# Expert routing in the first mixture of experts: dense products against rows sent to tiles of one expert

## The chip, the cores and the metric

The kernel runs on one core of a Trainium2 chip. The metric is the device time of one execution in microseconds. Half a dozen engines work side by side on one memory (SBUF): TensorE multiplies, VectorE and ScalarE read its results from the banks of PSUM (PB0 to PB7), Pool (GpSimd) helps, and SP issues transfers. They meet by counting semaphores.

## The reference

Four pairs of a convolution-like block and a token block work in turn on x of 8 images, 128 channels and 16x16 positions, that is 2048 tokens of 128 channels. The change is in the first token block, and touches nothing of what is computed. All is fp32.

```python
gate = jax.nn.softmax(xt @ Wg, axis=-1)            # 8 experts
topv, topi = jax.lax.top_k(gate, 2)
topv = topv / (jnp.sum(topv, axis=-1, keepdims=True) + 1e-06)
scores = jnp.zeros((T, E)).at[jnp.arange(T)[:, None], topi].set(topv)
for e in range(E):
    h = jax.nn.gelu(xt @ W1[e] + b1[e], approximate=False)   # 128 -> 512
    ye = h @ W2[e] + b2[e]                                   # 512 -> 128
    out = out + ye * scores[:, e:e + 1]
```

Here xt is the layer-normalised token, and the result is added to the unnormalised one. Two of the eight scores of a token are not zero.

## The kernel before

The tokens stand as 16 tiles of 128 tokens (X: a token on each partition, 128 channels in a row). Four tiles are a slot, and there are four slots. XT holds the normalised tiles, XN the same turned over, channels on the partitions.

First an upsampling and downsampling convolution runs through 28 steps c (TensorE L671 and L681; VectorE L1788, L1797, L1802 on each step). At c = 14, 21 and 28 and at the end VectorE adds a slot's result to X (finish, L1779) and takes its layer-norm statistics (L1688, L1691, L1694); Pool raises them to the power -1/2 (ln_pow, L475), VectorE normalises (L1711), TensorE turns the slot (ln_turn, L630) and ScalarE copies it out (ln_copy, L1352).

Then comes the expert stage. The logits of a token tile are one product with an 8-column matrix (L644). VectorE and ScalarE make scores of them for two slots at a time (router_start, router_act, router_finish: L1725 to L1755, with MAX8 in L1740 and MATCH_REPLACE8 in L1748), which land in comb, a column for each expert. TensorE goes through d = 0 to 31, expert d % 8 on slot d // 8. ffn_up(d) makes four products of 128x128 weights with the slot's 512 columns (L716); ScalarE does the gelu of each (L1402); ffn_down(d) makes, for each of the four token tiles, four 128x128 products (L727). ffn_up(d + 1) stands ahead of ffn_down(d) in the queue. VectorE adds each tile's result times its score to X (L1832), whatever the score is. All the experts' weights lie in SBUF, loaded in one piece at the start (stage1).

In between stand small pieces: the turned scores (comb_turn, L650), the b2 biases as products with them (expert_biases, L738), and the modulation of the next block (L765 to L776, bnrow and bt on ScalarE). After a slot's last expert VectorE takes the statistics for the next block and normalises it; Pool does the power and adds a row to X (shift, L492).

The next block begins with own_heads for three slots (L802, L809), and then takes the projection in which each product reads every sixteenth column of all 2048 tokens (L821). It so needs the last slot to be normalised, turned and copied.

SP issues every load: first (L432), x (L434), later, stage1 and mods (L435 to L437), and then the convolution weights of the later blocks into a ring of four buffers (L445, L447). Pool issues no transfer.

## Time and profile before

| What | us |
|---|---|
| median of 3 runs | 987.94 |
| lowest and highest run | 986.72, 990.4 |
| profiled execution | 988.28 |
| its span in the trace | 986.3 |
| TensorE busy | 842.2 |
| VectorE busy | 572.5 |
| ScalarE busy | 367.1 |
| Pool busy | 197.8 |

The mean granted clock of TensorE is 0.92 of full speed (2.4 GHz); the granted clock of a stretch is a column of the stage table. Busy times are of instructions; issuing a transfer is not in them. The profile names tiles without their numbers, and every tile in the big shared buffer is "arena". An fp32 product is recorded as two instructions. DMA moved 46 MB in 986 us, most of it in the first 40 us and in the two stretches with convolution weights.

### The profile page before, as it was taken

What the parts mean: (1) busy time and instruction counts of PE and PEld (TensorE: products, weight loads), DVE (VectorE), ACT (ScalarE), POOL (GpSimd) and SP (SyncE); (2) the same over time, 40 slices, a digit from 0 to 9 for tenths busy, and PEclk for the clock granted to TensorE, in tenths of its full rate; (3) what the DMA queues carried; (4) which work ended last, traced back from release to release, by engine and by line L of the source; (5) the groups of instructions that cost most, each with busy time, mean ns of one, the idle gap of its engine ahead of it and who ended that gap; (6) DMA issues with size and microseconds to landing.
All of it is one profiled execution on the core that took longest, in us unless ns stands there. A gap on an engine that the chain in (4) does not pass through costs nothing.

```text
span 986.3 us, 13502 instructions
## 1 busy us (share of the span) xinstructions
PE 842.2 (85%) x4689; PEld 636.1 (64%) x4689; DVE 572.5 (58%) x2105; ACT 367.1 (37%) x742; POOL 197.8 (20%) x258
## 2 busy tenths in 40 slices
PE   7999999999999999995866699878877677587868
PEld 5886777777777799985532588645555454363436
DVE  8984222122212345249576403369999989999773
ACT  1005434334333412220100112158868567465321
POOL 4101000010000100002011100235655544443300
PEclk9999999999999999996787799879988879788988
DMA  9600000000000035660000050000000002001020
GB/s 365 263 1 1 1 1 1 1 1 1 1 1 1 0 126 196 243 248 0 1 0 0 1 203 23 1 1 1 1 1 1 1 1 44 0 12 40 17 43 22
DMA packets 6739, 46.00 MB, mean 47 GB/s; under 512 B 632, under 2 KB 1656, under 8 KB 3984
## 3 DMA queue, kind: packets, MB, share of 16 engines
q1 hardware_dynamic: 6672, 45.14, 12.8%
q8 instruction: 38, 0.62, 0.3%
q14 instruction: 29, 0.24, 0.1%
HBM read 44.04 MB, written 1.10 MB: 46 GB/s over the span
## 4 chain that ended last, share of the span: by engine, by line
PE 62%; DVE 22%; issue 7%; POOL 5%; ACT 3%; DMA 0%; DVEq 0%; POOLq 0%; ACTq 0%
PE PB L727 12%; PE PB L716 11%; PE PB L843 5%; PE PB L1029 5%; DVE X L1962 3%; PE PB L681 3%; PE PB L671 3%; POOL arena L622 3%; PE PB L1207 2%; DVE arena L2213 2%; DVE top L2224 2%; PE PB L967 2%; DVE arena L2227 2%; DVE top L2208 2%; PE PB L630 1%
## 5 line engine op out<-in xcount | busy, mean ns | idle before, releaser
L1832 DVE SCALAR_TENSOR_TENSOR X<-PB,comb,X 128x128 f32<-128x128 f32 x128 | 36.0, 344 | 169.9 <-PE PB L727 169.9
L1402 ACT ACTIVATE arena<-PB,arena 128x512 f32<-128x512 f32 x128 | 87.4, 687 | 120.3 <-PE PB L716 120.1
L727 PEld LDWEIGHTS PB<-arena 128*128 128x128 f32 x1024 | 118.5, 192 | 11.0 <-issue 10.4
L727 PE MATMUL PB<-arena 128*128 128x128 f32 x1024 | 119.9, 276 | 0.0
L716 PE MATMUL PB<-XN,arena 128*128 128x512 f32 x256 | 115.6, 594 | 2.2 <-ACT arena L1402 2.2
L622 POOL TENSOR_TENSOR arena<-arena 128x512 f32<-128x512 f32 x64 | 81.3, 1271 | 120.9 <-ACT arena L1656 120.9
L475 POOL TENSOR_TENSOR lnrs<-lnve,mhalf 128x4 f32<-128x4 f32 x20 | 20.4, 1019 | 401.1 <-DVE lnve L1694 401.0
L1116 PE MATMUL PB<-ring 128*128 128x256 f32 x256 | 79.9, 442 | 16.7 <-ACT arena L1648 16.1
L1341 PE MATMUL PB<-w_first,arena 128*128 128x128 f32 x256 | 47.1, 314 | 46.0 <-POOL arena L622 45.6
L1656 ACT ACTIVATE arena<-arena,nmx 128x256 f32<-128x256 f32 x128 | 58.2, 506 | 57.5 <-DVE arena L2227 57.1
L1341 PEld LDWEIGHTS PB<-w_first,arena 128*128 128x128 f32 x256 | 33.2, 159 | 70.7 <-POOL arena L622 64.2
L716 PEld LDWEIGHTS PB<-XN,arena 128*128 128x128 f32 x256 | 46.1, 191 | 49.2 <-issue 44.6
L1116 PEld LDWEIGHTS PB<-ring 128*128 128x128 f32 x256 | 50.6, 219 | 29.8 <-issue 18.9
L1352 ACT ACTIVATE XN<-PB 128x512 f32<-128x512 f32 x20 | 11.9, 595 | 140.4 <-PE PB L630 140.4
L1648 ACT ACTIVATE arena<-PB,nmx 128x256 f32<-128x256 f32 x128 | 53.7, 477 | 5.8 <-DVE nmx L2214 3.8
L843 PE MATMUL PB<-arena,ring 128*128 128x128 f32 x480 | 55.8, 274 | 0.0
L2208 DVE MAX8 top<-PB 128x8 f32<-128x256 f32 x128 | 48.3, 418 | 12.7 <-PE PB L1116 12.6
L843 PEld LDWEIGHTS PB<-arena,ring 128*128 128x128 f32 x480 | 54.7, 190 | 0.0
L2213 DVE MATCH_REPLACE8 arena<-top,PB 128x256 f32<-128x256 f32 x128 | 51.9, 413 | 0.0
L2227 DVE MATCH_REPLACE8 arena<-top,arena 128x256 f32<-128x256 f32 x128 | 51.3, 408 | 0.0
L1029 PEld LDWEIGHTS PB<-arena,ring 128*128 128x128 f32 x392 | 47.5, 200 | 1.5 <-issue 1.5
L1029 PE MATMUL PB<-arena,ring 128*128 128x128 f32 x392 | 48.2, 285 | 0.0
(273 smaller groups left out, 1486.0 us busy)
## 6 DMA issues: line engine op xcount, KB each, us to landing
ring<-in_taps_dram SPq DMA_DIRECT2D x12, 1536.0 KB, 6.9
ring<-in_taps_dram SPq DMA_DIRECT2D x7, 1792.0 KB, 7.3
arena<-in_stage_dram SPq DMA_DIRECT2D x1, 4176.0 KB, 22.7
arena<-comb_rows SPq DMA_DIRECT2D x6, 512.0 KB, 6.2
w_later<-in_later_dram SPq DMA_DIRECT2D x1, 2951.5 KB, 13.3
XN<-in_x_dram SPq DMA_DIRECT2D x4, 256.0 KB, 4.9
out_dram<-XN SPq DMA_DIRECT2D x3, 256.0 KB, 2.2
arena<-in_mods_dram SPq DMA_DIRECT2D x1, 534.0 KB, 23.5
```

What stands on the lines that cost most here:

```text
L622: g.tensor_tensor(PR[c % 2], E1[c % 2], E2[c % 2], ALU.subtract).then_inc(sub_ready, 1)
L716: mm(PB[c % 3][:], W["W1"][:, e, hc * P:hc * P + P], xn(s), start=True, stop=True)\
L727: last = mm(PB[3 + d % 2][:, t * P:t * P + P], H[d % 2][hc][:, t * P:t * P + P], W["W2"][:, d % E, hc, :], start=hc == 0, stop=hc == 3)
L843: last = mm(PB[[3, 6][j % 2]][:, k * P:k * P + P].rearrange("p (b y) -> p b y", b=B), ring[:, j % T_RING, (6 * k + dy) * P:(6 * k + dy) * ...
L1029: last = mm(PB[1 + j % 2][:, k * P:k * P + P].rearrange("p (b y) -> p b y", b=B), ring[:, jj % T_RING, (7 * k + dy) * P:(7 * k + dy) * P + P],
L1116: last = mm(PB[c % 2][:, q * 256:q * 256 + 256], QM[c // 2 % 3][:, o + P * q:o + P * q + P], Kc[:, N * s + HW * j:N * s + HW * j + HW], st ...
L1341: last = tr(PB[3][:, kt * 256 + q * P:kt * 256 + q * P + P], PR[c % 2][:, q * 256 + kt * P:q * 256 + kt * P + P], ident)
L1402: A(H[d % 2][c % 4], PB[c % 3][:], ACT.Gelu, bias=W["b1"][:, c % 32:c % 32 + 1])\
L1656: last = A(E2[c % 2][:, q * 256:q * 256 + 256], REP[c % 2][:, q * 256:q * 256 + 256], ACT.Exp, bias=nmx[c % 4][:, q:q + 1])
L2208: k0 = [mark(v.max(t8[:, q, 0:8], lg[q])) for q in range(2)]
L2213: k.append(mark(v.match_replace(rp[q], t8[:, q, 0:8], lg[q], NEG)))
L2227: last = v.match_replace(rp[q], t8[:, q, 8:16], rp[q], NEG)
```

## The change

Routing is done before the products, and only the chosen experts' products are made. The 16 token tiles are handled as two halves of 8 tiles (two slots each). For each half:

1. pick_experts (VectorE) makes the softmax and finds the best and the second expert of each token as two 0/1 masks, and the two weights. Half 0's stands in the convolution's step c = 27, after logits at c = 20 and 25.
2. ranks (TensorE) counts, by nine products with a triangle of ones and with ones, how many rows before this one chose the same expert. ranks(0) stands after the upsampling steps and ahead of the downsampling left then; ranks(1) ahead of the first tile.
3. place_rows (VectorE, half 0 at c = 28) rounds each expert's count up to full tiles of 128 rows, and gives each of a token's two copies its row number, and each of the ROOM = 23 tiles its expert.
4. scatter (Pool) sends each token tile twice to DRAM, each row to its own row number: 16 indirect transfers for a half. ln_pow(1, 3) stands after the sixth. The DRAM buffers are zeroed by two transfers at the start.
5. SP reads the half's 23 tiles back in one transfer (rows_in), and for every tile reads its expert's number into a register and loads that expert's W1, W2 and b1 (128 x 1028 words) into one of four buffers (expert_weights).
6. For each of the 46 tiles TensorE turns the rows (four tiles or three together), makes four up products and four down products; ScalarE does four gelus of 128 columns. VectorE copies the turned rows and the results, a chunk of four tiles (the sixth of a half has three) at a time, and SP stores each chunk to DRAM.
7. gather (Pool) brings each token tile's two rows back by 16 indirect transfers for a half, and VectorE adds them with their weights (add_rows, 8 operations for a slot). Half 1's stand in two groups of 8, with ln_pow(2, 1) and the shift of slot 0 between, and the shift of slot 1 and the powers and shifts of slots 2 and 3 behind.

The scores in comb, the b2 biases, the modulation and all later stages stay. The loads of stage1 are gone, b2 moved to mods, and mods is loaded before later. Several semaphores of later stages are reused.

The core of the diff, with the repeated renaming left out:

```diff
+HALVES = 2
+HALF = NTOK // HALVES
+HT = HALF // P
+ROOM = 2 * HT + E - 1
+USES = HALVES * ROOM
+CHUNKS = [[list(range(ROOM * h + o, ROOM * h + min(o + 4, ROOM))) for o in range(0, ROOM, 4)] for h in range(HALVES)]
...
-            sp.dma_start(packs["stage1"], a["stage1"]).then_inc(stage1_in, 16)
+            def expert_weights(u):
+                h, i = divmod(u, ROOM)
+                sp.wait_ge(rows_placed, h + 1)
+                if u >= 4:
+                    sp.wait_ge(ffn_down_done, u - 3)
+                e = sp.value_load(tile_expert[0:1, h, i:i + 1], min_val=0, max_val=E - 1)
+                sp.dma_start(WB[u % 4], a["experts"][bass.ds(e, 1)].rearrange("e p w -> (e p) w"))\
+                  .then_inc(weights_in[u % 4], 16)
+
+            def rows_in(h):
+                sp.wait_ge(scattered[h], 2 * HT * 16)
+                sp.dma_start(XG[h], rows_there[h].rearrange("(i p) c -> p i c", p=P)).then_inc(xg_in[h], 16)
...
+            def first_experts():
+                for u in range(4):
+                    expert_weights(u)
+                rows_in(0)
+                for u in range(USES):
+                    if u + 4 < USES:
+                        expert_weights(u + 4)
+                    if u == ROOM - 6:
+                        rows_in(1)
+                    for q in range(len(CHUNKS)):
+                        if u == CHUNKS[q][-1]:
+                            rows_out(q)
...
+            def scatter(t):
+                h = t // HT
+                for k in range(2):
+                    g.indirect_dma_start(rows_there[h], bass.IndirectOffsetOnAxis(ap=row_number[:, h, k, t % HT:t % HT + 1], axis=0),
+                                         XT[:, t, :], None).then_inc(scattered[h], 16)
...
+            pool.wait_ge(zeroed, 16 * HALVES)
+            pool.wait_ge(rows_placed, 1)
+            for t in range(3):
+                scatter(t)
+            ln_pow(1, 3)
+            for t in range(3, HT):
+                scatter(t)
+            pool.wait_ge(rows_placed, 2)
+            for t in range(HT, NT):
+                scatter(t)
...
+            pool.wait_ge(y_stored[1], 16 * PER_HALF)
             pool.wait_ge(setup_act, 3)
+            for t in range(HT, HT + TILES):
+                gather(t)
+            ln_pow(2, 1)
             shift(0, 2, 0, bnrow[:, 1, :])
+            for t in range(HT + TILES, NT):
+                gather(t)
+            shift(0, 2, 1, bnrow[:, 1, :])
+            for s in range(2, SLOTS):
                 ln_pow(2, s)
                 shift(0, 2, s, bnrow[:, 1, :])
...
+            def ranks(h):
+                o = P + 72 * h
+                pe.wait_ge(mods_in, 16)
+                pe.wait_ge(experts_picked, h + 1)
+                m = picked2[:, h]
+                mm(PB[7][:, o:o + 72], W["rows_above"], m, start=True, stop=False)
+                for k in range(1, HT + 1):
+                    last = mm(PB[7][:, o + 8 * k:o + 72], ones[:], m[:, 0:72 - 8 * k], start=False, stop=k == HT)
+                last.then_inc(ranked, 1)
...
+            def ffn_up(u):
+                q = chunk_of(u)
+                i = CHUNKS[q].index(u)
+                pe.wait_ge(xgt_ready, q + 1)
+                pe.wait_ge(weights_in[u % 4], 16 * (u // 4 + 2))
+                if u >= 3:
+                    pe.wait_ge(ffn_gelu_done, u - 2)
                 for hc in range(4):
...
+                    last = mm(PB[u % 3][:, hc * P:hc * P + P], WB[u % 4][:, hc * P:hc * P + P],
+                              XGT[q % 3][:, i * P:i * P + P], start=True, stop=True)
+                last.then_inc(ffn_up_done, 1)
+
+            def ffn_down(u):
+                q = chunk_of(u)
+                i = CHUNKS[q].index(u)
+                pe.wait_ge(ffn_gelu_done, u + 1)
+                if q >= 2:
+                    pe.wait_ge(y_ready, q - 1)
+                for hc in range(4):
+                    last = mm(PB[3 + q % 2][:, i * P:i * P + P], H[u % 3][:, hc * P:hc * P + P],
+                              WB[u % 4][:, HID + hc * P:HID + hc * P + P], start=hc == 0, stop=hc == 3)
                 last.then_inc(ffn_down_done, 1)
```

## Rows read from the trace of the kernel before

**Rows 1.** The page: TensorE busy, with the other engines.

```profile
PE 842.2 (85%) x4689; PEld 636.1 (64%) x4689; DVE 572.5 (58%) x2105; ACT 367.1 (37%) x742; POOL 197.8 (20%) x258
```

**Rows 2.** Chain in order of time: start us, us, what.

```profile
70.25 6.91 PE PB L681 x32
77.60 1.69 PE PB L644 x16
...
150.19 3.57 PE PB L727 x32
153.76 3.44 PE PB L716 x8
...
328.65 10.71 PE PB L821 x32
...
395.32 1.75 PE PB L630 x16
```

**Rows 3.** Stage table: us, busy PE, PEld, DVE, ACT, POOL, clock, DMA share, GB/s.

```profile
78.00:320.00 242.00, 239.82 (x1398) 175.31 (x1398) 58.07 (x260) 99.59 (x148) 10.95 (x20) 1.00 0.00 1
```

**Rows 4.** Groups by form: shapes, count, busy us, mean ns, idle before.

```profile
L1402 ACT ACTIVATE arena<-PB,arena 128x512 f32<-128x512 f32 x128 | 87.4, 687 | 120.3 <-PE PB L716 120.1
...
L1832 DVE SCALAR_TENSOR_TENSOR X<-PB,comb,X 128x128 f32<-128x128 f32 x128 | 36.0, 344 | 169.9 <-PE PB L727 169.9
...
L492 POOL TENSOR_TENSOR X<-X,bnrow 128x128 f32<-128x128 f32 x16 | 6.8, 454 | 36.7 <-ACT bnrow L1393 33.0 <-DVE XT L1711 3.7
...
L1411 ACT ACTIVATE arena<-PB 128x256 f32<-128x256 f32 x8 | 3.1, 383 | 11.1 <-PE PB L802 11.1
```

**Rows 5.** Timeline, VectorE and Pool, 60 to 104 us: start us, us, what.

```profile
75.49 1.11 DVE L1711 TENSOR_SCALAR XT<-X,lnmv,lnrs 128x128 f32<-128x128 f32 x4 [1.12 <-POOL lnrs L475]
...
77.92 0.87 DVE L1688 BATCH_NORM_STATS2 lnst<-X 128x6 f32<-128x128 f32 x4
...
80.40 2.33 DVE L1711 TENSOR_SCALAR XT<-X,lnmv,lnrs 128x128 f32<-128x128 f32 x4 [1.12 <-POOL lnrs L475]
...
86.57 0.65 DVE L1740 MAX8 rt<-rt 128x8 f32<-128x8 f32 x8
...
87.59 0.08 DVE L1748 MATCH_VALUE_LOAD rt<-rt 128x8 f32 x1
...
88.61 0.15 DVE L1748 MATCH_REPLACE8 rt<-rt 128x8 f32<-128x8 f32 x1
...
80.31 1.77 POOL L529 MEMSET arena<- 128x640 f32 x3
```

**Rows 6.** Timeline, SP issuing queue, first 60 us: start us, us, what.

```profile
1.16 1.84 SPq L434 DMA_DIRECT2D XN<-in_x_dram  x4
```

**Rows 7.** DMA issues: count, KB each, median us to landing.

```profile
ring<-in_taps_dram SPq DMA_DIRECT2D x12, 1536.0 KB, 6.9
...
out_dram<-XN SPq DMA_DIRECT2D x3, 256.0 KB, 2.2
arena<-in_mods_dram SPq DMA_DIRECT2D x1, 534.0 KB, 23.5
w_first<-in_first_dram SPq DMA_DIRECT2D x1, 271.0 KB, 2.7
```

**Rows 8.** Groups by form, Pool.

```profile
L622 POOL TENSOR_TENSOR arena<-arena 128x512 f32<-128x512 f32 x64 | 81.3, 1271 | 120.9 <-ACT arena L1656 120.9
...
L475 POOL TENSOR_TENSOR lnrs<-lnve,mhalf 128x4 f32<-128x4 f32 x20 | 20.4, 1019 | 401.1 <-DVE lnve L1694 401.0
```

**Rows 9.** Stage table again, later windows, columns as in rows 3.

```profile
430.00:440.00 10.00, 8.44 (x62) 7.73 (x62) 5.89 (x19) 2.48 (x4) 0.00 (x0) 1.00 0.97 348
...
450.00:452.00 2.00, 0.00 (x0) 0.00 (x0) 2.00 (x1) 0.00 (x0) 0.18 (x1) 0.97 0.00 0
452.00:454.00 2.00, 0.87 (x4) 0.87 (x5) 1.93 (x5) 0.00 (x0) 0.00 (x0) 0.50 0.00 0
...
482.00:484.00 2.00, 1.96 (x7) 0.60 (x5) 1.90 (x18) 0.00 (x0) 0.00 (x0) 0.85 0.00 0
```

More of the change, by code:

```diff
@@ L719, in ffn_down @@
-            def ffn_down(d):
-                pe.wait_ge(ffn_gelu_done, 4 * d + 4)
-                if d < 2:
-                    pe.wait_ge(x_after_conv, 3 + d)
-                else:
-                    pe.wait_ge(ffn_added, d - 1)
-                for t in range(TILES):
-                    for hc in range(4):
-                        last = mm(PB[3 + d % 2][:, t * P:t * P + P], H[d % 2][hc][:, t * P:t * P + P],
-                                  W["W2"][:, d % E, hc, :], start=hc == 0, stop=hc == 3)
+            pe.wait_ge(*at(xn_ready[1], 2))
@@ new lines, in _, with chunk_of, turn_rows @@
+            ln_turn(1, 3, PB[6])
+            logits(0, 1, 2, W["Wg0"], PB[7])
+            logits(0, 1, 3, W["Wg0"], PB[7])
+            pe.wait_ge(x_after_conv, SLOTS)
+            def chunk_of(u):
+                return next(q for q, c in enumerate(CHUNKS) if u in c)
+            def turn_rows(q):
+                h = q // PER_HALF
+                if q == 0:
+                    pe.wait_ge(*at(xn_ready[1], 3))
+                else:
+                    pe.wait_ge(xgt_ready, q)
+                pe.wait_ge(xg_in[h], 16)
+                for i, u in enumerate(CHUNKS[q]):
+                    last = tr(PB[5][:, i * P:i * P + P], XG[h][:, u - ROOM * h, :], ident)
+                last.then_inc(xg_turned, 1)
@@ new lines, in place_rows @@
+            def place_rows(h):
+                o = P + 72 * h
+                tiles, start, end, first = [rank[:, 0, E * i:E * i + E] for i in range(4)]
+                dve.wait_ge(ranked, h + 1)
+                link(v.tensor_scalar(tiles, PB[7][:, o + 64:o + 72], 63.5, 1.0 / P, ALU.add, ALU.mult))
+                link(v.tensor_scalar(tiles, tiles, ROUND, -ROUND, ALU.add, ALU.add))
+                sums = rank[:, 1, 0:E * E].rearrange("p (a b) -> p a b", a=E)
+                link(v.tensor_tensor(sums, W["experts_below"], tiles.unsqueeze(1).to_broadcast([P, E, E]), ALU.mult))
+                link(v.tensor_reduce(start, sums, AX.X, ALU.add))
+                link(v.tensor_scalar(first, start, float(P), None, ALU.mult))
+                link(v.tensor_tensor(rank[:, 2, 0:HT * E].rearrange("p (t e) -> p t e", t=HT),
+                                     PB[7][:, o:o + 64].rearrange("p (t e) -> p t e", t=HT),
+                                     first.unsqueeze(1).to_broadcast([P, HT, E]), ALU.add))
+                link(v.tensor_tensor(rank[:, 3].rearrange("p (k n) -> p k n", k=2), picked[:, h],
+                                     rank[:, 2, 0:HT * E].unsqueeze(1).to_broadcast([P, 2, HT * E]), ALU.mult))
+                link(v.tensor_reduce(rank[:, 4, 0:2 * HT], rank[:, 3].rearrange("p (t e) -> p t e", e=E), AX.X, ALU.add))
+                v.tensor_copy(row_number[:, h].rearrange("p k t -> p (k t)"), rank[:, 4, 0:2 * HT])
+                link(v.tensor_tensor(end, start, tiles, ALU.add))
+                ahead = before.rearrange("p (i e) -> p i e", e=E)
+                link(v.tensor_tensor(ahead, W["tile_number"].unsqueeze(2).to_broadcast([P, ROOM, E]),
+                                     end.unsqueeze(1).to_broadcast([P, ROOM, E]), ALU.is_ge))
+                link(v.tensor_reduce(rank[:, 4, 2 * HT:2 * HT + ROOM], ahead, AX.X, ALU.add))
+                link(v.tensor_scalar(rank[:, 4, 2 * HT:2 * HT + ROOM], rank[:, 4, 2 * HT:2 * HT + ROOM], E - 1.0, None,
+                                     ALU.min))
+                v.tensor_copy(tile_expert[:, h], rank[:, 4, 2 * HT:2 * HT + ROOM]).then_inc(rows_placed, 1)
@@ new lines, in add_rows @@
+            def add_rows(s):
+                dve.wait_ge(gathered[s], 16 * 2 * TILES)
+                done = {}
+                for k in range(2):
+                    for t in range(TILES * s, TILES * s + TILES):
+                        if k:
+                            after(done[t])
+                        done[t] = mark(v.scalar_tensor_tensor(X[:, t, :], G[:, t, k, :],
+                                                              row_weight[:, t // HT, t % HT, k:k + 1], X[:, t, :],
+                                                              ALU.mult, ALU.add))
+                after(done[TILES * s + TILES - 1])
+                ln_stats(2, s)
@@ L1840, in _ @@
+            turned_rows(0)
+            for q in range(len(CHUNKS)):
+                if q + 1 < len(CHUNKS):
+                    turned_rows(q + 1)
+                rows_done(q)
+                if q < SLOTS:
+                    dve.wait_ge(fb_done, q + 1)
+                    k = mark(v.tensor_tensor(xf(q), xf(q), PB[6][:], ALU.add))
                     after(k)
                     v.nop().then_inc(fb_added, 1)
-                if d == 8:
-                    dve.wait_ge(mods_in, 16)
+                if q == 2:
```

466 lines of the change are left out of this document (268 added, 198 removed).

## The prediction

> **What bounds the kernel now.** I read the page first. TensorE is busy for 85% of the span and no other engine for more than 58% [rows 1], but that is a mean over eight stages, so I went to the chain in order of time for the first 460 us [rows 2]. From 70 us to 329 us it is TensorE nearly alone, and from 90 us on it repeats two pieces: 3.57 us of L727 (the down products of one expert on one slot) and 3.44 us of L716 (the up products of the next). There are 32 of each, with small insertions between them, and L821 begins at 328.65 us. The table by stage confirms it: from 78 to 320 us TensorE is busy 239.8 of 242 us at granted clock 1.00 (2.4 GHz), ScalarE 100 us, VectorE 58 us, Pool 11 us, DMA 1 GB/s [rows 3]. So this stage ends when TensorE has done its products, everything else hides in it, and the DMA engines are idle. Of the products three quarters are multiplied by a zero score.
>
> I compare everything at one point, the start of L821, which needs all four slots after the expert stage. It stands at 328.65 us; what follows is not changed but for renamed semaphores, and I cost that at nothing.
>
> **What goes.** 32 pairs, 32 x (3.44 + 3.57) = 224 us of TensorE, and beside them 128 gelus of 512 columns at 0.687 us and 128 VectorE additions of 0.344 us [rows 4]. The last two cost nothing today; TensorE covers them.
>
> **What comes, on TensorE.** A 128x128x128 product in fp32 is two instructions. L727 does 32 instructions in 3.57 us, so a product is 0.223 us. A tile of 128 rows now needs 4 up and 4 down products, 1.79 us, and a transpose, 0.11 us from the 16 of L630 in 1.75 us [rows 2]: 1.9 us. There are 46 tiles (23 in each half, since eight experts can each leave one tile part full), so 87 us instead of 224. The score turns, biases and the modulation products, about 9 us, stay. TensorE alone would need about 97 us.
>
> **What comes around it.** Rows must be sorted before the first tile and fetched back after the last. I follow the path.
>
> (a) *Picking, half 0.* It is put into the convolution's last steps on VectorE, and the rank products stand in TensorE's queue ahead of the last downsampling, so TensorE waits for it. VectorE needs eight MAX8 (0.65), sixteen pairs of value load and MATCH_REPLACE8 (eight of them stand between 87.59 and 88.76 us) [rows 5] and some nine small ops, which I put at 0.2 us each (an estimate from the 0.15 of one MATCH_REPLACE8 on 8 columns): about 5 us to the mask, after its own step at 72 us, so 77 us. The 18 rank instructions cost like the 16 of L644, 0.106 us each [rows 2], 1.9 us, or twice that since the clock will have fallen; done at 80.5. The downsampling of the last slot (6.9 us, L681 [rows 2], longer at the lower clock) then ends near 90 instead of 77 us. That is half 1's trouble and is hidden, for half 0 is not waiting for it. VectorE goes on with statistics (0.87 us [rows 5] and about 0.5 to gather them, 1.4) and fifteen small ops to place the rows, ready at about 85 us.
>
> (b) *Sending half 0.* Sixteen indirect transfers of 128 rows, issued by Pool one after another. The trace has no transfer issued by Pool. Nearest below is what SP's queue takes to issue one, 1.84 / 4 = 0.46 us [rows 6]; above I take the whole 2.2 us from issue to landing of a 256 KB store [rows 7], as if none overlapped. Pool's own instructions give 1.02 us for the power of 4 columns and 1.27 us for a 128x512 tensor op [rows 8]. I take 1.27, because addresses made in software resemble Pool work more than SP's. 16 x 1.27 + 1.0 (a power that stands between) = 21.3, to 106.3 us; landed (2.2) at 108.5.
>
> The Trainium skill, DMA: Bandwidth & Descriptors, Anatomy of one DMA, fits a Pool-issued transfer at 2.0 us and its bytes over 436 GB/s; for 64 KB an estimate of 2.15 us, if none overlapped. By that the sum would be 28 us higher. No run here shows it yet.
>
> (c) *Reading half 0.* SP fetches 23 tiles, 1.5 MB, only after all have landed. The tap loads are of that size, 6.9 us [rows 7]; these come in pieces of 512 bytes, I take 7.5: 116 us. Turn and copy (0.44 + 0.69 + waits): the first up product at 117.7 us.
>
> (d) *Weights.* Each tile has its own expert's 526 KB, loaded into four buffers. Tile u+4's load is issued when tile u's down products are done, so it has the time of four half steps, 4 x 0.893 = 3.6 us, to land. What it takes: a read of the expert's number into an SP register, which nothing here shows (from 0.1 to 2.7 us, the landing of the first pack; I take 1.3, between them), address and issue 0.5, landing 3.5 us (between 2.7 for 271 KB and 6.9 for 1536 KB [rows 7]). That is 5.3 us, late by 1.7, and four tiles share one turn: (5.3 + 3.6 + 0.3) / 4 = 2.3 us a tile. The floor is TensorE's 1.9. 46 x 2.3 = 106 us, at 229 GB/s; a stretch of tap loads ran at 348 GB/s [rows 9], so rate is no limit. ScalarE does four gelus of 128 columns, about 0.27 each from the 0.687 and 0.383 us of 512 and 256 columns [rows 4], 1.1 us a tile, under TensorE's. VectorE only copies, 2 x 0.69 us for four tiles. Half 1's picking, sending and reading lie under half 0's tiles (it has until 158 us and should land near 137). Add 4 us for the parts of the 9 that are not swallowed and 2 for a cold start. The last down product: 229.5 us.
>
> (e) *Fetching back.* Half 0's gathers are hidden. For half 1 the store of the last chunk lands at 233, then Pool issues 8 gathers, a power, four shifts (1.8, L492 [rows 4]), 8 gathers: 16 x 1.27 + 2.8, to 256.1, landed at 258.3. Behind them in Pool's queue stand the powers of slots 2 and 3, for which VectorE and then TensorE wait. VectorE applies slot 2, adds slot 3's rows (8 x 0.33) and its statistics (1.4), Pool's power 1.0, apply 1.1, turn and copy 1.5: L821 begins at about 267.7 us.
>
> (f) *Clock.* TensorE has nothing for some 20 us before its first tile and again at the gathers. In the trace, after a window without work (450 to 452 us), the clock read 0.50 (1.2 GHz) from 452 us, and 0.85 only in the window that begins at 482 us [rows 9]. I add 3 us for the second restart, as if about 6 us of its work ran at 1.2 GHz; by the 30 us of that row it could be 15.
>
> **Sum.** 328.65 - 267.7 = 61, less 3, gives 58 us. The profiled execution took 988.28 us (span 986.3), so 930. The median of the runs, 987.94, is the same within the scatter of 986.72 to 990.4. Thirty-two indirect transfers and forty-six tiles are the multipliers: a microsecond more in each moves the result by 32 or 46. Bounds: 0.46 us a transfer takes 26 off, tiles at 1.95 take 16 off, 888 together; 2.2 us a transfer adds 30, and 960.
>
> **Rivals.**
> *TensorE is the bound* (register read and landing fit into the slack): tiles at 1.95 us, 914; with transfers at 0.8 us, 899. For it: the DMA engines are idle and loads of this size could fly in threes. Chance 15%.
>
> *The weight loads are the bound.* If a load takes as long as a tap load of 1536 KB, because four are in flight beside the scatters, a turn is 6.9 + 1.3 + 3.9 over four, 3.0 us a tile: 34 us more, 964. For it: the stage's mods pack, queued behind others, took 23.5 us to land [rows 7]. Chance 20%. The Trainium skill, DMA: Bandwidth & Descriptors, Rules for kernel authors, speaks against loads this small: it wants 1 MiB and more, since the fixed part of each is paid again. By that rule this rival is the result; no load of this size is in the trace.
>
> *Pool is too slow at addresses, and the kernel ends slower.* Only the two serial trains of 16 decide, and the gain of 58 us is gone at 1.27 + 58 / 32 = 3.1 us a transfer; at 3.5 us the time is 1001. For it: VectorE and Pool disturb each other here, the four normalisations of a slot (L1711) took 2.33 us beside Pool's memsets (from 80.31 us) and 1.11 us otherwise [rows 5], and VectorE is active during both trains. Against: while the tiles run its reads are mostly from PSUM, and the disturbed op only doubled. Chance 6%. The Trainium skill, SBUF — State Buffer, two separate sides, gives such a rule: a Pool-issued transfer of 620 ns took 3100 ns beside a VectorE copy. By that rule this is the result, and the trace agrees in direction.
>
> *The clock falls in the tiles.* If TensorE, busy 1.9 of 2.3 us, is granted 0.50, a tile takes 3.8 us: 69 us more, 999. For it the 30 us at 0.50 above; against, 1.00 with 84% busy from 430 to 440 us [rows 9]. Chance 4%.
>
> **Chances.** Forecast 50%, TensorE-bound 15, weight-bound 20, Pool 6, clock 4, and 5 for mixtures that end near the old time. Half a per cent, 5 us, is about what these measurements can tell. Faster 0.86, same 0.04, slower 0.10. The range 900 to 975 leaves out the cheapest corner and the slower cases.
>
> **What would show it.** Right: the projection that follows (L821 now) starts near 268 us; Pool shows two trains of 16 at about 1.3 us each; the first up product near 118 us; tiles follow every 2.3 us with TensorE waiting for weight DMAs; clock 1.00 inside the tiles. Wrong: the trains at 2 us and more, tiles at 3 us with SP's register read in front, the wait before the last downsampling well above 10 us, or a clock of 0.5 in the tiles.

## The result and the profile after

The changed kernel takes 947.09 us (median of 4 runs, 942.53 to 949.14) beside 987.46 us of the kernel before on the same chip: ratio 0.958, 95% interval 0.954 to 0.962. Forecast were 930 us and a range of 900 to 975. The profiled execution of the changed kernel took 942.53 us, its span is 940.7, and the comparison is made with that one, as the prediction made it with 988.28.

The page of the changed kernel, the row that answers to [rows 1], and the row of the weight loads in its list of DMA issues (count, KB each, median us from issue to landing):

```profile
PE 734.5 (78%) x4227; PEld 578.5 (61%) x4227; DVE 570.7 (61%) x2109; ACT 326.7 (35%) x794; POOL 260.1 (28%) x323
...
arena<-in_experts_dram SPq DMA_DIRECT2D x46, 514.0 KB, 4.5
```

TensorE lost 107.7 us of busy time (842.2 to 734.5) and the kernel 45.8. It is now busy for 78% of the span, not 85.

The lines have moved: the up product L716 is L865, the down product L727 is L876, the transpose of rows is L854, the projection L821 is L958. The chain of waits of the changed kernel in order of time, which answers to [rows 2] (start us, us, what):

```profile
79.35 3.32 PE PB L827 x16
...
87.05 1.25 POOL rows_there L612
88.30 0.30 issue
88.61 0.96 POOL rows_there L612
...
106.12 0.96 POOL rows_there L612
...
107.39 2.23 DMA rows_there<-XT,row_number
...
109.69 8.03 DMA arena<-rows_there
...
117.85 1.10 PE PB L854 x4
...
119.72 3.79 PE PB L865 x16
```

and its end, from the last tile to the projection:

```profile
248.71 2.07 DMA rows_back<-arena
...
272.68 0.94 POOL arena L618
...
273.65 1.68 POOL X L575 x4
275.32 1.02 POOL lnrs L558
...
276.37 1.13 DVE XT L1847 x4
...
286.03 4.24 PE PB L958 x12
```

The chain has fifteen transfers of Pool; the sixteenth is issued at 107.39, and from there the chain goes on with the transfer itself. In place of one even row of products there are now three pieces behind the picking: 33 us of sending and reading (87.05 to 119.72), where TensorE has little to do, 128.4 us of tiles to 248.09, and 37.9 us of fetching back to 286.03. The stage table has one row for the tiles (columns as in [rows 3], where TensorE was busy 239.82 of 242 us at 1.00 and the DMA engines moved 1 GB/s):

```profile
120.00:248.00 128.00, 110.14 (x849) 103.72 (x849) 22.22 (x52) 54.77 (x192) 29.61 (x33) 0.94 0.73 223
```

TensorE is idle for 17.9 of 128 us, its granted clock is 0.94, not 1.00, and the DMA engines, idle before, are busy for 73%. The waits of that stage (engine, line, what it waited for: us in total, times, longest) have no releaser that the profile could name ("issue"); that they are waits for weights is shown by e2_no_loads, below:

```profile
PE PB L865 <- issue: 17.4, 24, 1.9
```

After the projection nothing was changed, and it takes 654.7 us (940.7 - 286.03) in place of 657.65 (986.3 - 328.65).

### The profile page after: what moved, and what is told of

Same layout as the page of the kernel before. It is cut to its first block, busy times and chain, and to the rows that moved or that the text cites. A ratio compares the mean times of both kernels' runs of the same rounds, so it can differ in the third digit from the quotient of the medians.

```text
span 940.7 us, 12950 instructions
## 1 busy us (share of the span) xinstructions
PE 734.5 (78%) x4227; PEld 578.5 (61%) x4227; DVE 570.7 (61%) x2109; ACT 326.7 (35%) x794; POOL 260.1 (28%) x323
## 4 chain that ended last, share of the span: by engine, by line
PE 51%; DVE 30%; issue 7%; POOL 6%; ACT 4%; DMA 2%; DVEq 0%; POOLq 0%; ACTq 0%; SPq 0%
PE PB L980 6%; PE PB L865 6%; PE PB L1166 5%; PE PB L876 5%; DVE arena L2442 3%; DVE X L2191 3%; DVE top L2453 3%; PE PB L786 3%; DVE top L2437 3%; DVE arena L2456 2%; PE PB L796 2%; PE PB L1344 2%; PE PB L1104 2%; POOL arena L618 2%; POOL rows_there L612 2%
## 5 line engine op out<-in xcount | busy, mean ns | idle before, releaser
L1253 PE MATMUL PB<-ring 128*128 128x256 f32 x256 | 76.4, 426 | 17.4 <-ACT arena L1784 16.8
L1534 ACT ACTIVATE arena<-PB,arena 128x128 f32<-128x128 f32 x184 | 52.2, 365 | 73.2 <-PE PB L865 73.2
L865 PE MATMUL PB<-arena 128*128 128x128 f32 x368 | 54.6, 296 | 18.3 <-issue 17.4
L1253 PEld LDWEIGHTS PB<-ring 128*128 128x128 f32 x256 | 48.7, 211 | 29.5 <-issue 18.8
L865 PEld LDWEIGHTS PB<-arena 128*128 128x128 f32 x368 | 48.4, 206 | 23.0 <-issue 19.9
L980 PE MATMUL PB<-arena,ring 128*128 128x128 f32 x480 | 55.7, 274 | 0.0
L980 PEld LDWEIGHTS PB<-arena,ring 128*128 128x128 f32 x480 | 54.7, 190 | 0.0
L745 PE MATMUL PB<-w_first,XT 128*128 128x128 f32 x80 | 18.1, 369 | 45.3 <-DVE XT L1847 44.9
L876 PE MATMUL PB<-arena 128*128 128x128 f32 x368 | 51.7, 286 | 0.3 <-ACT arena L1534 0.3
L618 POOL DMA_INDIRECT arena<-rows_back,row_number x32 | 30.6, 955 | 72.0 <-DMA rows_back<-arena 63.0
L2042 DVE COPY arena<-PB 128x512 f32<-128x512 f32 (+1 forms) x12 | 8.0, 669 | 66.6 <-PE PB L876 66.6
L876 PEld LDWEIGHTS PB<-arena 128*128 128x128 f32 x368 | 47.2, 200 | 1.4 <-ACT arena L1534 0.5
```

Source lines behind the costliest of these rows:

```text
L865: last = mm(PB[u % 3][:, hc * P:hc * P + P], WB[u % 4][:, hc * P:hc * P + P], XGT[q % 3][:, i * P:i * P + P], start=True, stop=True)
L876: last = mm(PB[3 + q % 2][:, i * P:i * P + P], H[u % 3][:, hc * P:hc * P + P], WB[u % 4][:, HID + hc * P:HID + hc * P + P], start=hc == 0, ...
L980: last = mm(PB[[3, 6][j % 2]][:, k * P:k * P + P].rearrange("p (b y) -> p b y", b=B), ring[:, j % T_RING, (6 * k + dy) * P:(6 * k + dy) * ...
L1253: last = mm(PB[c % 2][:, q * 256:q * 256 + 256], QM[c // 2 % 3][:, o + P * q:o + P * q + P], Kc[:, N * s + HW * j:N * s + HW * j + HW], st ...
L1534: last = A(H[u % 3][:, hc * P:hc * P + P], PB[u % 3][:, hc * P:hc * P + P], ACT.Gelu, bias=WB[u % 4][:, 2 * HID + hc:2 * HID + hc + 1])
```

## The experiments

Marks of the profiled executions; "tiles" is from the first up product to the end of the last down product, "tail" from there to the projection, "rest" from there to the end of the span. A ratio is to the kernel before on the same chip.

| kernel | first up | tiles | tail | projection | rest | median us | ratio, 95% interval |
|---|---|---|---|---|---|---|---|
| forecast | 117.7 | 111.8 | 38.2 + 3 | 270.7 | 657.7 | 930 | |
| changed | 119.7 | 128.4 | 37.9 | 286.0 | 654.7 | 947.1 | 0.958 (0.954 to 0.962) |
| e1_again | 119.5 | 128.0 | 37.8 | 285.3 | 663.9 | 945.0 | 0.954 (0.947 to 0.960) |
| e2_no_loads | 119.4 | 101.2 | 37.3 | 257.9 | 659.9 | 918.9 | 0.928 (0.921 to 0.935) |
| e3_six_buffers | 120.2 | 106.1 | 37.9 | 264.1 | 653.6 | 919.7 | 0.932 (0.924 to 0.940) |
| e4_half_trains | 113.1 | 124.7 | 27.5 | 265.3 | 662.4 | 930.3 | 0.940 (0.934 to 0.946) |
| e5_shifts_last | 119.5 | 127.4 | 37.0 | 283.8 | 661.2 | 946.8 | one run |
| e6_kept_busy | 119.8 | 131.5 | 38.3 | 289.6 | 661.4 | 953.0 | one run |
| e7_ranks_late | 119.9 | 128.6 | 38.3 | 286.8 | 662.0 | 950.6 | one run |
| e8_best | 115.0 | 103.1 | 37.0 | 255.1 | 659.3 | 916.3 | 0.928 (0.925 to 0.932) |
| e9_three_buffers | 120.2 | 184.5 | 37.9 | 342.6 | 653.6 | 998.0 | one run |
| e10_best_plain | 115.1 | 104.7 | 37.9 | 257.7 | 650.3 | 916.6 | 0.929 (0.924 to 0.934) |
| e11_best_warm | 117.6 | 107.4 | 37.8 | 262.8 | 660.1 | 923.2 | 0.932 (0.926 to 0.938) |

The stages up to the projection repeat within a microsecond (changed and e1_again, the same code). The rest does not: it runs from 650.3 to 663.9 in kernels that are alike there. So the stages are read at the projection, and the totals are left for what is larger than some 10 us. Where the table says one run, marks and time are of a single execution.

**e1_again.** The changed kernel unchanged.

> The changed kernel once more, to stand beside the next three on one chip. Every theory: 940 to 950 us, first up product near 120 us, last down product near 248 us, 2.8 us a tile.

Measured 945.01 us (940.37 to 951.03), and the marks of the table. The miss against 930 is no accident of one execution.

**e2_no_loads.** Only the first four tiles load weights; the other 42 use what lies in the four buffers, so their products are of the wrong experts. Nothing else is left out; the stores of a half wait for each other.

```diff
                 if u >= 4:
                     sp.wait_ge(ffn_down_done, u - 3)
+                    return
                 e = sp.value_load(tile_expert[0:1, h, i:i + 1], min_val=0, max_val=E - 1)
...
-                pe.wait_ge(weights_in[u % 4], 16 * (u // 4 + 2))
+                pe.wait_ge(weights_in[u % 4], 32)
```

> Only the first four tiles' weights are loaded, every later tile uses those four buffers again; SP keeps its waits. The results are not the reference's. Theory A, the tiles wait for their weights: up products start with no wait, about 2.0 us a tile plus 8 us of other products, some 102 us for the stage instead of 128, total about 920. Theory B, the handshake of TensorE with ScalarE's gelus and VectorE's copies sets the 2.8 us: no change, 942 to 947. Theory C, the clock: with the waits gone the granted clock should be 1.00 from 126 us to the end of the stage.

Measured: tiles in 101.2 us, 27.2 less. The stage table of 100 us of it:

```profile
120.00:220.00 100.00, 99.66 (x845) 97.44 (x844) 22.23 (x52) 54.76 (x192) 28.63 (x33) 0.97 0.21 64
```

TensorE has no gap left, and this is its own price for 46 tiles with all that stands between them: 2.2 us a tile. The 27 us of the changed kernel above it are then 17.9 us of gaps and some 9 us in which TensorE is busy for longer with the same products (110.14 in place of 101). These 9 us have two parts. A clock that is either 1.00 or 0.50 and reads 0.94 on average over 128 us was at half for about 15 us, against 6 us here; the trace puts 13.5 us of the changed kernel's products at half clock and 5.9 us of this one's, which costs some 4 us. And an up group that starts behind a gap stands in the chain with 1.13 us, one that follows without a gap with 0.89. The second can be seen in the changed kernel at 178.26 (its chain), the first in the chain under (d) below:

```profile
178.26 0.89 PE PB L865 x8
```

With 24 gaps that is 24 x 0.24, 6 us. The clock goes with the gaps: 0.97 here, 0.94 in the changed kernel, 0.85 in e9_three_buffers below. Here it is at half only in the first 6 us of the tiles.

**e3_six_buffers.** Two more weight buffers, which take the place of the padded buffers of a later stage (they are cleared behind the last tile, for that). All else is as in the changed kernel.

```diff
-                if u >= 4:
-                    sp.wait_ge(ffn_down_done, u - 3)
+                if u >= 6:
+                    sp.wait_ge(ffn_down_done, u - 5)
...
-                sp.dma_start(WB[u % 4], a["experts"][bass.ds(e, 1)].rearrange("e p w -> (e p) w"))\
+                sp.dma_start(WB[u % 6], a["experts"][bass.ds(e, 1)].rearrange("e p w -> (e p) w"))\
...
```

> Six weight buffers instead of four, in room that is dead while the tiles run; Pool clears the padding buffers after the last tile instead of before the first. Theory A1, the latency of a load with too few in flight: with down(u) behind up(u+1) in the queue, n buffers give (L + 1.8) / (n - 1) a tile; L = 6.1 us gives 2.6 for four and 1.6 for six, so TensorE's 2.0 to 2.1 us sets the pace, stage near 104 us, total about 922. Theory A2, the rate of the DMA engines: a load takes longer in proportion, the tiles stay at 2.6 to 2.8 us, total 940 to 947.

Measured: tiles in 106.1 us, and a median of 919.66 us (916.85 to 928.67). The same loads, of the same bytes, 46 of them, and 22 of the 27 us are back. What remains is in part one wait: the rows of half 1 are asked for at tile 17 and land behind the queued weights. Timeline of TensorE in e3_six_buffers (start us, us, engine, line, operation, tile, the idle time before with what ended it):

```profile
173.20 1.06 PE L868 MATMUL PB<-arena 128*128 128x128 f32 x8
176.89 0.63 PE L857 MATMUL PB<-w_first,arena 128*128 128x128 f32 x4 [2.63 <-DMA arena<-rows_there]
```

**e9_three_buffers.** One buffer fewer, to tell two forms of the cadence apart.

```diff
-                if u >= 4:
-                    sp.wait_ge(ffn_down_done, u - 3)
+                if u >= 3:
+                    sp.wait_ge(ffn_down_done, u - 2)
...
-                sp.dma_start(WB[u % 4], a["experts"][bass.ds(e, 1)].rearrange("e p w -> (e p) w"))\
+                sp.dma_start(WB[u % 3], a["experts"][bass.ds(e, 1)].rearrange("e p w -> (e p) w"))\
...
```

> Three weight buffers in place of four: tile u+3's weights are issued when tile u's down products are done. By the theory (up(u+1) stands in TensorE's queue ahead of down(u), so a buffer's round trip covers n-1 tiles) a tile takes (L + 1.8) / 2; with L, from a buffer free to weights landed, 0.9 + 4.5 = 5.4 to 6.1 us, that is 3.6 to 3.95 us a tile, and the tile stage 166 to 182 us in place of 128; the last down product starts at 285 to 301 us, total 980 to 998. The rival is the prediction's own form, (L + 3.9) / n with n buffers: 3.1 to 3.3 us a tile, stage 143 to 152, last down product at 262 to 271, total 957 to 967. If rate in flight sets L (three loads land faster than four), both lie at their lower ends.

Measured 998.0 us in its one run, above all seven runs of the kernel before beside it (984.4 to 992.7); tiles in 184.5 us, 4.0 us a tile. Its stage table, and its load of the weights in the list of DMA issues:

```profile
120.00:304.00 184.00, 128.19 (x845) 120.24 (x846) 22.33 (x53) 54.76 (x192) 30.01 (x34) 0.85 0.53 158
```

```profile
arena<-in_experts_dram SPq DMA_DIRECT2D x46, 514.0 KB, 3.7
```

The form with n buffers in the denominator allowed 152 us at most and is out. The form with n - 1 came nearer, 2.5 us short at its upper end, but the landing, 3.7 us with fewer loads in flight, was shorter than it assumed: with 3.7 it gives (4.6 + 1.8) / 2 = 3.2 us a tile, the form with n (4.6 + 3.9) / 3 = 2.8. What decides between them is a stretch at full clock. The up groups of TensorE's timeline start at 158.19 and, two tiles later, at 165.22: 7.0 us, of which 0.9 are a turn of rows and one of scores, so 3.1 us a tile. The next two tiles, in part at half clock, take 9.2 us (to 174.44). What the form leaves out is thus the lower clock (in the row above, at 0.85, TensorE's own 101 us became 128), the insertions, and one wait of 6.5 us for a load that was issued beside the read of half 1's rows and took 9.3 us to land.

**e4_half_trains.** Each row is sent to and fetched from its first expert only, 8 transfers in each train in place of 16; its second expert's row is not computed, and the first is added twice. The 46 tiles stay.

```diff
-                for k in range(2):
+                for k in range(1):
                     g.indirect_dma_start(rows_there[h], bass.IndirectOffsetOnAxis(
...
-                for k in range(2):
+                for k in range(1):
                     g.indirect_dma_start(G[:, t, k, :], None, rows_back[h],
...
```

> Only the first of a token's two rows is sent and fetched: 8 indirect transfers in each train instead of 16; VectorE adds the first row twice. The results are not the reference's. Theory: Pool's issue at 1.26 us each is the path, so 8 fewer before the first tile and 8 fewer after the last give 20 us less, about 927, with the first up product near 110 us. Rival: landing and reading back set the path, less than 5 us gained.

Measured: the projection 20.7 us earlier: 10.4 of it in the tail (37.9 to 27.5), 6.6 ahead of the first tile and 3.7 in the tiles, for which no run shows a cause. Behind the tiles the train stands on the path with its full length, as the prediction had it. In front, eight transfers of 1.26 us are 10.1, and the first up product came at 113.1, not near 110. Pool waits 2.21 us for VectorE's variances in the middle of the train, and then something else ends last. TensorE's timeline of e4_half_trains:

```profile
109.27 1.09 PE L854 MATMUL PB<-w_first,arena 128*128 128x128 f32 x4 [0.37 <-DMA arena<-rows_there]
113.13 3.78 PE L865 MATMUL PB<-arena 128*128 128x128 f32 x16 [2.77 <-DVE arena L2034]
```

The rows were turned at 109.27, but VectorE's copy of them (L2034) stands in its queue behind the placing of half 1's rows, which waits for half 1's rank products and ends near 112.5. In the changed kernel that placing is done at 114.8 and the copy starts at 118.97: half 1's picking is hidden there by no more than 4.2 us. By the chain of the changed kernel above, a transfer is 0.96 us of Pool and 0.30 us of issue: 1.26 us, forecast 1.27.

**e5_shifts_last.** Pool's four shifts behind the powers for which VectorE waits.

```diff
             ln_pow(2, 1)
-            shift(0, 2, 0, bnrow[:, 1, :])
             for t in range(HT + TILES, NT):
                 gather(t)
-            shift(0, 2, 1, bnrow[:, 1, :])
-            for s in range(2, SLOTS):
-                ln_pow(2, s)
-                shift(0, 2, s, bnrow[:, 1, :])
+            ln_pow(2, 2)
+            shift(0, 2, 0, bnrow[:, 1, :])
+            ln_pow(2, 3)
+            for s in range(1, SLOTS):
+                shift(0, 2, s, bnrow[:, 1, :])
```

> Pool's four shifts go behind the powers of slots 2 and 3, nothing else is moved. Theory, Pool's queue is the path after the last tile: the second train of eight ends 1.7 us earlier and slot 2's power follows at once, so the projection L958 starts about 3.3 us sooner after the last down product ends than in the changed kernel (there 248.1 to 286.0, 37.9 us; here 34.6). Rival, the arithmetic of VectorE and TensorE is the path there: the distance stays within 0.5 us.

Measured: the tail is 0.9 us shorter. The timelines of e5_shifts_last say where the rest went, Pool first, then VectorE:

```profile
262.27 2.52 POOL L618 DMA_INDIRECT arena<-rows_back,row_number  x1 [0.30 <-issue]
...
272.31 1.04 POOL L558 TENSOR_TENSOR lnrs<-lnve,mhalf 128x4 f32<-128x4 f32 x1
273.34 1.67 POOL L575 TENSOR_TENSOR X<-X,bnrow 128x128 f32<-128x128 f32 x4
```

```profile
261.77 2.18 DVE L2051 SCALAR_TENSOR_TENSOR X<-arena,row_weight,X 128x128 f32<-128x128 f32 x8
...
273.39 2.22 DVE L1847 TENSOR_SCALAR XT<-X,lnmv,lnrs 128x128 f32<-128x128 f32 x4 [8.04 <-POOL lnrs L558]
...
280.23 1.71 DVE L1847 TENSOR_SCALAR XT<-X,lnmv,lnrs 128x128 f32<-128x128 f32 x4 [1.13 <-POOL lnrs L558]
```

The power of slot 2 comes at once behind the last gather (272.31, not behind a shift of 1.68 us), 1.8 us sooner behind the last down product than in the changed kernel, where 3.3 were expected. But then the normalisation L1847 and the shift run side by side, and L1847 takes 2.22 and 1.71 us, where the changed kernel had 1.12 at both places; and one gather took 2.52 us as VectorE's additions began. e10_best_plain, below, is the counterpart.

**e6_kept_busy.** 14 products of constants, never read, ahead of the first turn of rows and ahead of the last slots' turn.

```diff
             ranks(1)
+            for i in range(14):
+                mm(PB[4][:, 0:P], ident, ones[:], start=True, stop=True)
             turn_rows(0)
...
```

> Fourteen idle products (about 6 us at half clock) are put where TensorE waits for the first tile, and fourteen more where it waits for slot 2; their results are not read. Theory, the clock at 1.2 GHz costs time on the path: the first tiles at full clock, 2 to 3 us less before 130 us, and turn, own_heads and the last turn in about 4 us less before the projection. Rival: the clock does not come back in either stretch, and the time stays or grows by up to 1 us.

Measured: no gain, the projection at 289.6 in place of 286.0. The windows of 10 us around the first tile, the changed kernel and then e6_kept_busy:

```profile
110.00:120.00 10.00, 2.57 (x11) 2.10 (x12) 3.74 (x15) 0.00 (x0) 3.83 (x4) 0.50 0.63 170
120.00:130.00 10.00, 10.00 (x69) 9.78 (x70) 0.69 (x1) 5.00 (x17) 7.65 (x8) 0.78 0.37 112
```

```profile
110.00:120.00 10.00, 8.13 (x42) 7.73 (x43) 3.75 (x15) 0.00 (x0) 3.38 (x4) 0.67 0.61 170
120.00:130.00 10.00, 9.96 (x72) 9.51 (x73) 0.69 (x1) 5.00 (x17) 7.55 (x9) 0.84 0.42 131
```

The clock is up from 0.50 to 0.67 and from 0.78 to 0.84, but the first up product came no earlier (119.8) and the tiles were waiting for weights. Of the 3.6 us that the projection came later 3.1 are in the tiles, where the clock reads 0.92 on average against 0.94; with one run it is open whether the idle products did that. The second set did not reach its aim: it ran at 273.98 to 277.27, and TensorE then had nothing for 4.50 us.

**e7_ranks_late.** The rank products of half 0 behind the remaining downsampling, not ahead of it.

```diff
-            ranks(0)
             for s, i in todo:
                 downsample(s, i)
+            ranks(0)
```

> The rank products of half 0 stand behind the rest of the downsampling instead of ahead of it. Theory: the wait of TensorE for the picking (5.6 us before L825) is not on the path, since half 1 has slack, while half 0's placing is: rows placed 1 to 3 us later, and everything to the projection later by as much. Rival, the early ranks cost time because they hold back the last slot: the first tile comes earlier or the stage gets shorter.

Measured: first up product at 119.9, projection at 286.8, in place of 119.7 and 286.0, so neither theory's microseconds: half 0's first scatter begins at 87.20 in place of 87.05. TensorE's 5.64 us of waiting for the picking (row under (a) below) cost nothing, and sparing them gained nothing.

**e8_best.** The six buffers; the rows of half 1 asked for at tile 9; of half 0's rows the first four tiles in a transfer of their own; Pool's order of e5_shifts_last.

```diff
-                    if u == ROOM - 6:
+                    if u == 9:
                         rows_in(1)
...
+                if h == 0:
+                    sp.dma_start(XG[h][:, 0:4, :], rows[:, 0:4, :]).then_inc(x_loaded[2], 16)
+                o = 4 if h == 0 else 0
+                sp.dma_start(XG[h][:, o:, :], rows[:, o:, :]).then_inc(xg_in[h], 16)
```

> Six buffers (e3), half 1 read back at tile 9 instead of 17, half 0's first four tiles read by a transfer of their own, shifts last (e5). Theory: on e3's projection start of 264.2 us, the 10 us gap before half 1 goes, the split read gives 3 to 4 us, the shifts 3 us: about 248 us, total near 905. Rival, the DMA engines are the bound once tiles run at 2 us beside the reads: 255 us or more, total 912 and up.

Measured 916.3 us (913.8 to 920.34), ratio 0.928 (0.925 to 0.932): 30.8 us below the changed kernel's 947.1. The first up product comes 4.7 us earlier, and the wait for half 1's rows is gone. The expected 248 and 905 us were missed by 7 and 11. Against e3_six_buffers the split read and what goes with it gave 5.2 us, the earlier read of half 1 3.0 in the tiles where 10 were put down, and Pool's order 0.9 in place of 3. The numbers are the rival's, 255 and 912 or more, but not its cause: TensorE is idle for 1.8 of the 103 us of tiles, so it is the bound there and not the DMA engines. In front the first tile now waits for what e4_half_trains showed, VectorE's copy behind the placing of half 1's rows. TensorE's timeline of e8_best:

```profile
115.02 3.78 PE L875 MATMUL PB<-arena 128*128 128x128 f32 x16 [2.06 <-DVE arena L2044]
```

That placing ends at 114.4 here. Putting the copy, or the first turn of rows, ahead of half 1's picking was not tried.

**e10_best_plain** and **e11_best_warm.** The first is e8_best with Pool's order of the changed kernel, the second adds both sets of 14 products.

> As e8_best, but with Pool's order behind the tiles as in the changed kernel (each shift where it was). In e5_shifts_last and e8_best one gather took 2.52 us beside VectorE's additions, and the next normalisation 2.2 us beside the shift. If the later shifts give nothing because Pool and VectorE stretch each other, this kernel lies within 2 us of e8_best (914 to 920); the rival is that the new order still gave its 1 to 3 us, so 917 to 923. Last down product near 218 us, projection 37 to 38 us later.

> e10_best_plain with the two sets of 14 idle products on TensorE, ahead of the first turn of rows and behind the last tile's copy (their results are not read). In e6_kept_busy the weight loads set the pace, so a better clock in front had nothing to give; here six buffers leave TensorE as the bound. If the cold start costs here, the first 10 us of tiles go from a granted clock near 0.5 to near 1.0 and 2 to 4 us are gained (912 to 916). The rival: the first tiles still wait for their weights and rows and the second set stands too early in time to help the projection, so no difference within 2 us.

Measured: 916.62 and 923.21 us. Pool's new order gives 0.9 us in the tail (37.0 and 37.9) and nothing that the totals show. Either is the best version found: 31 us below the changed kernel, 71 below the kernel before. e11_best_warm is 6.6 us slower, where 2 to 4 us less or no difference were expected. The idle products cost 2.5 us at the first tile: they ended at 116.4, while in e10_best_plain the rows had landed and were being turned at 112.1. The tiles took 2.7 us more, for which no run shows a cause. TensorE's timeline in e10_best_plain and in e11_best_warm:

```profile
115.08 3.79 PE L875 MATMUL PB<-arena 128*128 128x128 f32 x16 [1.85 <-DVE arena L2044]
```

```profile
111.05 5.33 PE L899 MATMUL PB<-ones,w_first 128*128 128x128 f32 x28
...
117.60 2.05 PE L875 MATMUL PB<-arena 128*128 128x128 f32 x16 [0.78 <-DVE arena L2049]
```

The two first up groups took 2.05 us in place of 3.79, so the cold start costs 1.7 us there, less than the products that end it. With six buffers the DMA engines are busy all the time where weights, stores and Pool's gathers come together, and TensorE even so has no gap; two windows of e10_best_plain:

```profile
190.00:200.00 10.00, 10.00 (x91) 9.91 (x90) 2.02 (x4) 6.16 (x23) 7.56 (x9) 1.00 1.03 377
200.00:210.00 10.00, 10.00 (x91) 10.00 (x91) 1.78 (x3) 5.70 (x20) 1.59 (x2) 1.00 1.00 358
```

Ten loads of weights were issued in these 20 us, 5.3 of the 7.4 MB moved, so about 263 GB/s are weights.

## Why the prediction was right in its sign, and where it was short

Its point, the projection, came at 286.0 and not at 270.7: 15.3 us later; the rest was 3.0 us shorter, which is chance, since that stage runs from 650.3 to 663.9 us; 930 + 15.3 - 3.0 = 942.3, the profiled 942.5. (By the medians the miss is 17 us, within the range given.) Point by point:

*(a) Picking* was forecast with the mask at 77 and the ranks at 80.5 us; L827 ended at 82.67 and the first scatter began at 87.05, forecast 85. The downsampling left then took 8.46 us to 90.97, forecast 90. TensorE's wait was 5.64 us, and e7_ranks_late shows it hidden. That half 1's picking is hidden too holds by 4.2 us alone (e4_half_trains).

```profile
78.68 0.67 PE L825 MATMUL PB<-arena 128*128 128x72 f32 x2 [5.64 <-DVE arena L1923]
82.51 8.46 PE L796 MATMUL PB<-arena 126*128 126x256 f32 x28
```

*(b) Sending* was right: 1.26 us each, the last one issued at 107.39 and landed at 109.6 (forecast 108.5). That it came to the 1.27 of a 128x512 tensor operation is luck in part: the price has two pieces, 0.96 us of Pool, near its small power of 1.02 [rows 8], and 0.30 between two. The Trainium skill, DMA: Bandwidth & Descriptors, Anatomy of one DMA, would have put 28 us on top. Its fixed part is there, since a transfer to DRAM lands 2.23 us after its issue, but the next is issued after 1.26: latency, not occupancy, and e4_half_trains prices a transfer on the path at 10.4 / 8 = 1.3 us.

*(c) Reading half 0* took 8.03 us in place of 7.5, and the first up product came at 119.7 in place of 117.7. e8_best reads what the first four tiles need by itself and starts them 4.7 us earlier.

*(d) Weights* is the step that failed: "(5.3 + 3.6 + 0.3) / 4 = 2.3 us a tile". Measured 128.4 / 46 = 2.79, with insertions; forecast 111.8 / 46 = 2.43 with them. That is 16.6 us. With 2.0 more in front, and 3.3 fewer behind than the 38.2 + 3 put down, it makes the 15.3 at the projection. Of the inputs, the register read was dearer in the forecast (1.3 us) than on the chip (0.27 us and 0.15 us for its two instructions, 0.8 us in all from a down product's end to the issue), and the landing was 4.5 us at the median in place of 3.5 (3.3 at the least, 5.2 in the stretch below, beside the gathers); together they nearly made up for each other at the median, but not beside other traffic. The forecast called a load of this size absent from the trace; the mods pack of 534 KB [rows 7] was one, though queued behind others. What was wrong in kind was the turn. The chain of waits of the changed kernel, with the issues of the queue that reads weights beside it, tells it:

```profile
199.24 0.89 PE PB L876 x8
200.14 0.31 issue
200.45 1.13 PE PB L865 x8
201.58 0.89 PE PB L876 x8
202.47 1.06 issue
203.53 1.13 PE PB L865 x8
204.66 0.44 PE PB L854 x4
205.09 0.89 PE PB L876 x8
205.99 1.03 issue
207.02 1.13 PE PB L865 x8
208.15 0.89 PE PB L876 x8
```

```profile
200.94 0.34 SPq L492 DMA_DIRECT2D arena<-in_experts_dram  x1
```

Call the down product (L876) at 199.24 that of tile v. It ends at 200.13, the load of tile v+4 into its buffer is issued at 200.94, and up(v+4) (L865) starts at 207.02, 6.9 us behind that end (this load took 6.0 us to land). TensorE works in order, and up(u+1) stands ahead of down(u): behind up(v+4) comes down(v+3), which ends at 209.04 and only then frees the next buffer of this turn. From down(v) to down(v+3) are 8.9 us for three tiles, 2.97 each: the round trip, from a buffer free to the products that wait for it (L) and then an up and a down group, is shared by n - 1 tiles, not by n. Here that is (6.9 + 1.13 + 0.89) / 3 = 2.97. With L = 0.8 + 4.5 to 5.2 + 0.1 = 5.4 to 6.1 us it is (5.4 to 6.1 + 1.8) / 3 = 2.4 to 2.6 us without the insertions; the forecast's form gives 2.3 to 2.5 for the same L. With six buffers it is at most 7.9 / 5 = 1.6, below TensorE's 1.9, and the bound goes back to TensorE (e3_six_buffers, e8_best); with three it is 3.2, and e9_three_buffers shows it at full clock.

How the 16.6 us divide can only be estimated from these numbers. The form is worth about 0.1 us a tile with four buffers, 3 to 6 us (with three it is 0.4, which is why e9_three_buffers can tell). The longer round trip of the loads is worth 1 to 9 us. The rest is what the forecast had at nothing: products behind a gap that take 0.24 us longer a group and the part at half clock (9 us of TensorE together, not all of it on the path), and one collision. SP asks for half 1's rows at 172.91, the load issued at 175.49 takes 8.4 us to land in place of 4.5, and TensorE's two longest waits of the stage, 1.6 and 1.9 us, end at 176.24 and 183.95.

*(e) Fetching back* was forecast at 38.2 us from the last down product and measured at 37.9. (The pieces that the forecast lists behind the landing at 258.3 add up to 8.7 us, not to the 9.4 that lead to 267.7.) *(f) Clock*: the windows from 250 to 290 us read 0.54 to 0.76, but TensorE's work there is short. The 3 us added for it were not needed in the tail. In the tiles the forecast had 2 us for a cold start, and e10_best_plain beside e11_best_warm shows 1.7; what it had at nothing is the clock falling again behind the gaps of (d).

*The rivals.* "TensorE is the bound" (914) is what e2_no_loads, e3_six_buffers and e8_best show once the buffers are there; not this kernel. "The weight loads are the bound" (3.0 us a tile, 964) was the nearest, its 2.79 between that and the forecast, but for another reason: not the bytes, since the same bytes in e8_best go through in 103 us. The rule for loads of 1 MiB and more that the prediction cites with that rival (the Trainium skill, DMA: Bandwidth & Descriptors, Rules for kernel authors) is not what decides here: in the two windows above the DMA engines moved 358 to 377 GB/s, no transfer larger than 514 KB among them, against 348 in a stretch of tap loads of 1536 KB [rows 9]. "Pool is too slow" is out with 1.26 us. The lock that the Trainium skill, SBUF — State Buffer, two separate sides, describes shows in none of the 32 gathers of the changed kernel (0.94 to 1.06 us, VectorE's copies from PSUM and its additions beside them); whether the one of 2.52 us in e5_shifts_last is such a case is open. "The clock falls in the tiles" is out as priced: the clock read 0.94, and the part at half clock cost some 4 us, not 69.

## What to carry to other kernels

Where TensorE issues the next tile's first product ahead of this tile's last one, a ring of n buffers gives a load the time of n - 1 tiles, less the two half steps that frame it; write one buffer's round trip down with the queue's order in it before dividing. Gaps of TensorE cost more than their length (here 18 us of them brought 9 us more, some 6 of it in groups that start behind a gap and some 4 at half clock), so a buffer more than the sum asks for is cheap. Row by row transfers from Pool cost 1.26 us each for 128 rows where they stand in a serial train; hide the trains, or make the first consumer need fewer of them, and look for what ends last once they are shorter: here it was the placing of the other half, 4.2 us behind.

## What the runs showed that was not expected

The end of the kernel, the same code in all, took from 650.3 to 663.9 us, and the changed kernel alone 654.7 and 663.9. The same 50 us of it, 450 us behind the projection, in the changed kernel and in e1_again:

```profile
736.00:786.00 50.00, 34.42 (x192) 23.37 (x190) 47.98 (x212) 35.46 (x86) 24.83 (x28) 0.97 0.03 7
```

```profile
735.00:785.00 50.00, 37.99 (x185) 26.54 (x185) 45.15 (x200) 32.72 (x79) 25.96 (x27) 0.80 0.00 1
```

The granted clock was 0.97 in the one and 0.80 in the other, with TensorE at work for 34 and 38 of the 50 us. What tips it was not tried.

A normalisation on VectorE (four TENSOR_SCALAR from X to XT) took 1.12 us by itself and 2.2 us with Pool's additions to X beside it, as in the 2.33 us beside Pool's memsets of [rows 5]; in the changed kernel it is slot 1's that takes 2.23 us, and reordering Pool's work put the cost on the others. And one gather of 32 took 2.52 us in e5_shifts_last and in e8_best (2.00 in e6_kept_busy and e7_ranks_late), as VectorE's additions began, where all of the changed kernel and of e10_best_plain stayed at 1.06 or less; what decides it is open.
